# Reordering the last gates, halving the first attention input, and idle products at the start of a two-stage fp32/bf16 layer

## The reference

```
x = x + mamba_block(norm(x))      # norm, rmsnorm, in_proj, conv, scan with 16 states, gate, out_proj, FFN
x = x + gated(norm(x))            # recurrence over the 8 entries of the batch, then tanh
x = x + attention(norm(x))        # 16 heads of width 16; scores = (x_h W_h) x_h^T / 4
x = x + gated(norm(x))            # same weights as the first

def gated(x):                     # x[b] is 512 x 256, b = 0..7 in order
    for b in range(8):
        f, i = sigmoid(x[b] wf + c uf + bf), sigmoid(x[b] wi + c ui + bi)
        c = f * c + i * tanh(x[b] wc + c uc + bc)
    return tanh(x wo + c uo + bo)  # c is the last state
```

## Time and profile before

| | us |
|---|---|
| median of 3 runs | 1643.46 |
| lowest, highest | 1641.68, 1645.18 |
| profiled execution | 1647.02 |
| span of the profiled execution (first to last instruction) | 1645.2 |

### The profile page before, as it was taken

The page is one execution under the profiler, slowest core; times in us unless marked ns, Lnnn a source line. Parts: engine busy times, 40 slices in busy tenths (PEclk is TensorE's granted clock), DMA queues, the critical chain, the costliest instruction groups (busy, mean ns, idle before and its releaser), DMA issues.

```text
span 1645.2 us, 17272 instructions
## 1 busy us (share of the span) xinstructions
PE 1373.9 (84%) x5520; PEld 661.9 (40%) x5520; DVE 1183.2 (72%) x1824; ACT 884.9 (54%) x1512; POOL 689.7 (42%) x402
## 2 busy tenths in 40 slices
PE   4224789999999998999837989999999999989994
PEld 1102344545353635465411334444444443434442
DVE  3598898989898988950249777676767676666325
ACT  4664858585857574522211565646465555545533
POOL 2577879787878776730343121212030212100000
PEclk9666889999999999999965999999999999999997
DMA  5516060606161515100344433323243332320044
GB/s 177 179 40 205 28 230 28 230 28 217 41 205 53 192 53 179 52 32 8 102 95 100 73 95 78 79 54 86 57 97 73 84 76 55 85 53 15 15 157 137
DMA packets 93786, 158.04 MB, mean 96 GB/s; under 512 B 8592, under 2 KB 74704, under 8 KB 90576
## 3 DMA queue, kind: packets, MB, share of 16 engines
q1 hardware_dynamic: 93696, 156.94, 33.1%
HBM read 110.91 MB, written 46.01 MB: 95 GB/s over the span
## 4 chain that ended last, share of the span: by engine, by line
PE 62%; DVE 20%; issue 10%; ACT 4%; POOL 2%; DMA 1%; SPq 0%; DVEq 0%; POOLq 0%; ACTq 0%
PE psum L973 25%; PE psum L1860 8%; PE psum L1794 7%; PE psum L1768 7%; PE psum L1743 6%; PE psum L1783 5%; DVE psum L538 5%; DVE mx L1284 4%; PE psum L1018 2%; DVE middle L500 1%; DVE hb L538 1%; DVE stats L1260 1%; DVE hb L541 1%; PE psum L1738 1%; DVE bg_stats L468 1%
## 5 line engine op out<-in xcount | busy, mean ns | idle before, releaser
L1284 DVE TENSOR_REDUCE mx<-psum 128x1 f32<-128x512 f32 x512 | 344.9, 687 | 192.6 <-PE psum L1768 189.6
L1535 ACT ACTIVATE pw<-psum 128x512 f32<-128x512 f32 x512 | 301.9, 598 | 303.5 <-PE psum L1783 300.8
L910 POOL TENSOR_TENSOR hb<-ddb,bcb 128x1024 f32<-128x1024 f32 x128 | 309.8, 2443 | 65.5 <-DVE middle L500 52.3
L538 DVE TENSOR_TENSOR_SCAN psum<-psum,hb 128x512 f32<-128x512 f32 x224 | 261.5, 1213 | 29.7 <-ACT psum L729 18.1
L1768 PE MATMUL psum<-kp,qp 96*128 96x512 bf16 x512 | 209.2, 410 | 48.8 <-DVE mx L1284 30.0
L729 ACT ACTIVATE psum<-ddb,A_neg 128x512 f32<-128x512 f32 x256 | 165.4, 682 | 79.7 <-DVE hb L541 60.2
L1783 PE MATMUL psum<-qp,kp 99*128 99x512 bf16 x512 | 199.6, 391 | 7.8 <-ACT pw L1535 6.2
L1679 POOL TENSOR_TENSOR rstd<-rstd,neg_half 128x4 f32<-128x4 f32 x16 | 16.3, 1018 | 448.9 <-DVE rstd L1269 448.9
L541 DVE TENSOR_TENSOR hb<-psum,bcb 128x1024 f32<-128x1024 f32 x112 | 137.2, 1225 | 3.9
L1794 PE MATMUL psum<-pw,v_sb 128*32 128x512 f32 x1024 | 133.3, 641 | 0.5 <-ACT pw L1535 0.5
L973 PE MATMUL psum<-back,w 128*128 128x512 f32 x256 | 115.3, 605 | 8.3 <-ACT back L745 8.3
(11 more groups left out here) (189 smaller groups left out, 2166.9 us busy)
## 6 DMA issues: line engine op xcount, KB each, us to landing
ddb<-dd SPq DMA_DIRECT2D x64, 512.0 KB, 6.7
bcb<-bc SPq DMA_DIRECT2D x32, 512.0 KB, 6.7
parts<-parts_sb SPq DMA_DIRECT2D x96, 128.0 KB
dd<-dd_out SPq DMA_DIRECT2D x8, 1024.0 KB, 4.8
qp<-parts SPq DMA_DIRECT2D x32, 256.0 KB, 8.0
kp<-parts SPq DMA_DIRECT2D x16, 384.0 KB, 4.5
x_front<-x_dram SPq DMA_DIRECT2D x8, 512.0 KB, 4.2
xh<-x_front SPq DMA_DIRECT2D x8, 512.0 KB, 5.6
```

The lines of the kernel that those rows point to most:

```text
L538: e.tensor_tensor_scan(to[:, g, :], a[:, g, :], h[:, g, :], 0.0, ALU.mult, ALU.add).then_inc(scan_ok, 1)
L910: e.tensor_tensor(hb[n % NHB], ddb[k % NSLOT][:, 1:2, :].to_broadcast([P, 2, L]), bcb[q][:, 0, :, :], ALU.mult).then_inc(bx_ok, 1)
L1284: used.up(e.tensor_reduce(mx[u % 2][:, n:n + 1], bank(used.n % 2), AXIS.X, ALU.max))
L1535: e.activation(pw[n % NPW], bank(5 + n % 2), ACT.Exp, scale=HD ** -0.5).then_inc(exp_ok, 1)
```

## The change

There are four groups of edits.

1. Last gates. In round 8 the product gc of entry 6 comes after both halves of `back_second` in place of before them (TensorE, the ring's order, and VectorE, whose `gate_in` moves from u = 11 to u = 14 behind `back_new`). In round 9 `gate_xwo` of entry 7 is no longer ahead of the gates: its first half follows gf, its second half follows `final_state`; `last_gate_in` makes gi with the x terms of both halves first. ScalarE's copies and SP's store follow, so that the last `xwo1` store is issued in stage two, between `x_load(0)` and `x_load(1)`.
2. First attention input. `final_state` writes banks 0 and 1; cuo, xw, tanh, x2 and its moments of entry 0 go in two halves of two token tiles each. The wait for stage one's last stores moves behind them (`first_free`, and the end of `first_tanh`).
3. First q and k parts. All four steps of each (k, q) x (f = 0, 1) are done on VectorE in the order k0, q0, k1, q1 (`first_parts`), and SP sends and fetches one f after the other: 6 sends of f = 0, fetch(0), 6 sends of f = 1, fetch(1). GpSimd does none of them; its `front_bias(0)` and `restart` move into p = -2.
4. Idle products. `stay_warm(n)` does n fp32 products of 128 x 512 into bank 4, used by nothing: 8 at the very beginning, 2 after z of entry 0, 18 after dt of entry 0.

```
 # first_uses
-        if gate:
+        if gate and i != NB:
             use("dve", "gc", i - 2, 2)
         if back:
             use("dve", "ffn_out", i - 1, 2)
+        if gate and i == NB:
+            use("dve", "gc", i - 2, 2)
         if gate:
             use("dve", "gf", i - 2, 2)
+        if i == NB + 1:
+            use("act", "xwo", i - 2, 2)
...
 # pe_first
+            def stay_warm(n):
+                for _ in range(n):
+                    e.matmul(bank(4), ident, rows_flat[:, 0:L], start=True, stop=True)
+            def last_gate_in(b):
+                ring_out(e, "gturn", b, 1)
+                w = lambda f: slice(D + f * P, D + (f + 1) * P)
+                for f in range(NF):
+                    ring_free(e, "gi", b, f)
+                    for j in range(NF):
+                        e.matmul(ring("gi", b, f), wx[:, j, w(f)], feat(X0)[:, j, :], start=j == 0, stop=False)
+                e.wait_ge(c_new, b)
+                for f in range(NF):
+                    for j in range(NF):
+                        ins = e.matmul(ring("gi", b, f), uh[:, j, w(f)], c_state[:, j, :], start=False, stop=j == NF - 1)
+                    ins.then_inc(r_pe, 1)
+            stay_warm(8)
...
+                if i == -1:
+                    stay_warm(2)       # after mid_in z
...
+                if i == -1:
+                    stay_warm(18)      # after mid_dt
...
-                if gate:
+                if gate and i != NB:
                     gate_one(i - 2, "gc", 2)
...
+                if gate and i == NB:
+                    gate_one(i - 2, "gc", 2)   # after back_second(i - 1, 1)
                 if gate:
                     gate_one(i - 2, "gf", 0)
+                if i == NB + 1:
+                    ring_free(e, "xwo", i - 2, 0)
+                    token_product(ring("xwo", i - 2, 0), 0, feat(X0), wo).then_inc(r_pe, 1)
...
 # sp_second
+            def first_send(f):
+                for n in (1, 0):
+                    for c in range(3):
+                        if f == 0:
+                            e.wait_ge(first_part, 3 * (1 - n) + c + 1)
+                        elif c < 2:
+                            e.wait_ge(cast_ok, (0 if n else 2) + c + 1)
+                        else:
+                            e.wait_ge(sub_ok, 2 if n else 4)
+                        e.dma_start(part_dram[0][n, f, c]..., parts[n][:, c, f]).then_inc(part_sent[2 * n], 16)
             x_load(0)
+            ring_out(e, "xwo", NB - 1, 1)
+            e.dma_start(rows_of(xwo1_dram[NB - 1]), tok(G2)).then_inc(xwo1_sent[(NB - 1) % 2], 16)
             x_load(1)
-            for p in range(-4, NU):
+            for f in range(NF):
+                first_send(f)
+                fetch(f)
+            for p in range(-2, NU):
...
 # dve_second
             for u in range(2):
+                tiles = slice(2 * u, 2 * u + 2)
                 e.wait_ge(cuo_pe, u + 1)
-                e.tensor_tensor(cuo[:, 2 * u:2 * u + 2, :], halves(bank(5 + u)), ...).then_inc(cuo_ok, 1)
+                e.tensor_tensor(cuo[:, tiles, :], halves(bank(u)), ...).then_inc(cuo_ok, 1)
+                e.wait_ge(cuo_ok, u + 1)
+                e.wait_ge(xwo_in[0], 16)
+                e.tensor_tensor(xw[0][:, tiles, :], xw[0][:, tiles, :], cuo[:, tiles, :], ALU.add).then_inc(xc2_ok, 1)
...
+            def first_parts(n, f):
+                src, left = feat(A1 if n else A2)[:, f, :], feat(H1 if n else H0)[:, f, :]
+                misc_out(e, ("turn" if n else "q", 0, f))
+                ...
+                done(e.tensor_copy(part(0), src), cast_ok)
+                ins = e.tensor_tensor(left, src, part(0), ALU.subtract)
+                done(e.tensor_copy(part(1), left), cast_ok)
+                done(e.tensor_tensor(part(2), left, part(1), ALU.subtract), sub_ok)
...
                 if p == -3:
-                    first_cast(1, 0)
-                    first_cast(1, 1)
-                    first_cast(0, 0)
-                    first_sub(1)
-                    first_cast(0, 1)
-                    first_sub(2)
+                    for f in range(NF):
+                        first_parts(1, f)
+                        first_parts(0, f)
...
 # pool_second
+                if p == -2:
+                    front_bias(0)              # after front_xw(1)
...
-                if p == -3:
+                if p == -2:
                     restart()
...
 # pe_second
-            final_state((5, 6))
+            final_state((0, 1))
+            ring_free(e, "xwo", NB - 1, 1)
+            token_product(ring("xwo", NB - 1, 1), 1, feat(X0), wo).then_inc(r_pe, 1)
```

More of the change, by code:

```diff
@@ L402, in sp_first @@
                     e.dma_start(x_back, x_tile(b)).then_inc(x_back_in, 16)
-                if gate:
+                if gate and i <= NB:
                     ring_out(e, "xwo", i - 2, 1)
@@ L619, in dve_first @@
                         gated(i, 0)
-                    if u == 11 and gate:
+                    if u == 11 and gate and i != NB:
                         gate_in(i - 2)
@@ L623, in dve_first @@
                         back_new(i - 1)
+                    if u == 14 and i == NB:
+                        gate_in(i - 2)
                     if u == 15 and gate:
@@ L800, in act_first @@
                         gate_turned(i - 2)
-                    if u == 2 and gate:
+                    if u == 2 and gate and i <= NB:
                         gate_xwo(i - 2)
@@ L842, in act_first @@
                         gate_f(i - 2)
+                    if u == 15 and i == NB + 1:
+                        ring_done(e, "xwo", i - 2, 0)
+                        e.activation(tok(G2)[:, 0:2, :], halves(ring("xwo", i - 2, 0)), ACT.Copy).then_inc(r_act, 1)
                     if u == 15 and front:
@@ new lines, in first_stats, with first_free @@
+            def first_stats(k):
+                e.wait_ge(own.sem, own.n)
+                spread(x2[0], 0, k)
+            def first_free():
+                for i in range(2):
+                    e.wait_ge(x1_sent[i], 16 * NB // 2)
+                    e.wait_ge(xwo1_sent[i], 16 * NB // 2)
+            def first_parts(n, f):
+                src, left = feat(A1 if n else A2)[:, f, :], feat(H1 if n else H0)[:, f, :]
+                misc_out(e, ("turn" if n else "q", 0, f))
+                part = lambda c: parts[n][:, c, f, :]
+                done = lambda ins, sem_: ins.then_inc(first_part if f == 0 else sem_, 1)
+                at = (first_part, 3 * (1 - n)) if f == 0 else (cast_ok, 0 if n else 2)
+                done(e.tensor_copy(part(0), src), cast_ok)
+                e.wait_ge(at[0], at[1] + 1)
+                ins = e.tensor_tensor(left, src, part(0), ALU.subtract)
+                if f == 0:
+                    own.up(ins)
+                    e.wait_ge(own.sem, own.n)
+                else:
+                    ins.then_inc(sub_ok, 1)
+                    e.wait_ge(sub_ok, 1 if n else 3)
+                done(e.tensor_copy(part(1), left), cast_ok)
+                e.wait_ge(at[0], at[1] + 2)
+                done(e.tensor_tensor(part(2), left, part(1), ALU.subtract), sub_ok)
@@ L1622, in act_second @@
                         cast(b + 2, 0, 0, s - 18)
-                    if s == 19 and not odd and front:
+                    if s == 19 and not odd and front and b + 2 > 0:
                         front_tanh(b + 2)
+                    if s == 19 and p == -4:
+                        first_tanh()
                     if s == 22 and odd and gate:
```

99 lines of the change are left out of this document (47 added, 52 removed).

## The result

| | before | after |
|---|---|---|
| median of the runs, us | 1644.32 (1641.68 to 1647.71, 4 runs) | 1629.08 (1627.25 to 1631.91, 4 runs) |
| profiled execution, us | 1647.02 | 1629.72 |
| its span, us | 1645.2 | 1627.9 |

The ratio after to before is 0.9904, with a 95% interval of 0.9887 to 0.9920: 0.96% faster, 15.2 us by the medians. Forecast was 1626, a gain of 17.05.

A forecast was written before the change was run, and what follows sets the result against it. Chains of waits in the opening and the joint of the two stages, with PE mostly idle, bound the edited places. -4.6 - 2.45 - 1.5 + 0.3 - 9.3 + 0.5 = -17.05 took the median 1643.46 to 1626; range 1620 to 1636.

The forecast's parts named there:

- Opening: Start to entry 1's transposition: idle products raise the clock, so transposition, input products and xp run faster, -4.6 us.
- rival (a): Opening: clock not up at entry 0's transposition, by late products or a short idle time; opening gains 0, 1631; chance 0.09.
- (d): Opening: clock stays slow throughout, so the idle products are in the way; slower, 1648.6; chance 0.04.
- +0.95: Round 8: moving gc of entry 6 uncovers the last relu, PE waits before `back_second`, nothing won; +0.95 us.
- -3.4: Round 9: taking xwo from the front removes 5.0 us, but gi inherits 1.6 of slow clock; -3.4 us.
- Halves: Final state to T, start of the first attention input's transposition: work in two halves on VectorE shortens it; -1.5 us.
- the counted 0.3: Before T: VectorE waits for the last xwo1 store before writing the normalized input; +0.3 us.
- Parts and fetch: T to first score: parts on VectorE alone, f = 0 sent and fetched first; 18.8 us for 28.1, -9.3.
- 7.0 + 0.5: Fetch of f = 0: 7.0 us from q's first issue to landing, plus 0.5 for six sends queued behind.
- rival (b): Fetch bound by bytes and sends, not the queue behind; 5.5 for 9.3, store landing late 1.4; 1631.6; chance 0.08.
- Restart: Behind the first score: `restart` on GpSimd runs beside entry 1's normalization on VectorE; +0.5 us, bounds 0 and +3.
- Rival (c): First unit's scores: something else is late and takes the gain back; 1635.7, or 1638.9 for the whole joint; chance 0.07.

The follow-up runs named there:

- the best version: Kernel after with gc of entry 6 ahead of `back_second` again and idle products: 3 before the last gate transposition, 6 before T, 9 before the first score; 1624.37 us, ratio 0.9881.
- The kernel that holds everything back: Kernel after, but SP holds the six sends of f = 1 until all of q of f = 0 has landed; 1629.96 us, ratio 0.9913.

## Why the prediction was right

**Opening: right in size and in place.** -4.67 for -4.6. By the rule of the Trainium skill (TensorE: Matmul & The Clock Gate, Part 1: The HAM clock gate) the number of slow matmuls at a start varies, and its largest number would have given 3.5. Here about 6 of the first block were slow, fewer than the 8 to 10 that I took. That starts vary is borne out: in the twelve profiles with this block it took 8.62 to 10.21 us, so 4 to 8 of the 16 were slow, and it was always done before the transposition, by 0.38 to 2.89 us. In two of the twelve the input products behind the transposition then ran partly slow, and entry 1's transposition came at 59.5 in place of 58; these are the two with the longest waits ahead of the transposition, 2.29 and 2.89 us. So it looks as if rival (a)'s mechanism, a short idle time that drops the clock, did come in these two, for 1.5 us. The timelines of the best version, twice:

```profile
21.62 8.80 PE L986 MATMUL psum<-front,w_in 128*128 128x512 f32 x16 [1.01 <-ACT front L669]
```

```profile
21.71 7.10 PE L986 MATMUL psum<-front,w_in 128*128 128x512 f32 x16 [1.01 <-ACT front L669]
```

The 18 products, cost nothing and bring nothing: right. For the kernel after rivals (a) and (d) fell.

**Last gates: the step that failed is the price of moving gc, "+0.95".** What the uncovered relu costs was right (+1.04, in the timeline after as PE's wait of 0.78 us):

```profile
757.12 1.13 PE L990 MATMUL psum<-w,back 128*128 128x256 f32 x4 [0.78 <-ACT gate L760]
```

But the move has a second price that the prediction put at nothing, the clock behind PE's last wait. In the kernel after the last transposition was slow (1.69 for 1.09), and so were about six of gi's eight x products, (6.07 - 3.43) / 0.43. The clock was at the lower level until it rose between 794 and 796:

```profile
790.00:792.00 2.00, 1.96 (x3) 0.93 (x4) 0.00 (x0) 0.00 (x0) 0.26 (x1) 0.50 0.00 0
...
794.00:796.00 2.00, 2.00 (x5) 0.76 (x4) 0.00 (x0) 0.00 (x0) 0.00 (x0) 0.79 0.03 8
```

The order of gc decides it. In all six profiles with gc moved that transposition took 1.57 to 1.69, in the three with gc at its old place and nothing added to the wait 1.09. With gc back gi took 5.19, about four of the eight slow, that is 1.76 us of slow clock where I had let it inherit 1.6, and the final state came 26.92 behind the transposition in place of 30.33: 3.41 less. So the "-3.4" for taking xwo away was right by itself. Moving gc cost 1.04 + 1.42 = 2.46 for the forecast 0.95, and the two together brought 0.95 us for 2.45. With three idle products in the wait gi took 3.70. PE's wait ahead of the transposition is 2.74 us with gc in either place; why the order of the same products before it changes the clock behind it wasn't taken apart and stays open.

**Halves: right.** -1.67 up to T, for -1.2 with the store. The store of xwo's half landed at 822.37 + 3.37 = 825.74, just when VectorE had its normalization ready to start (825.96), so the counted 0.3 did not appear:

```profile
825.96 1.38 DVE L1336 TENSOR_SCALAR attend<-x,mv,rstd 128x256 f32<-128x256 f32 x4 [1.39 <-POOL rstd L1762]
```

No run has the halves alone. In the kernel with the idle products alone, which lacks them, the final state to T took 13.14, in the kernel after 11.48.

**Parts and fetch: the direction right, the size 1.7 too large.** The chain of copies was right: last send at T + 7.73 (7.9), landed at T + 11.1 (11.3). The step that failed is the fetch's 7.0 + 0.5, read from the fetch at 904.69 because that "had none behind it". From q's first issue at 838.63 to the first score it took 9.37 us, as before (9.4); that was rival (b)'s mechanism, at a third of its price, since the store landed in time and the six sends cost nothing. My argument had been that seven fetches queued behind q cost 2.4 us. The kernel that holds everything back shows that q takes as long with nothing behind it, 9.59. The trace of the kernel before had a row that said so too, which I did not look at: the fetch at 974.57, with k 1.28 us ahead of it and nothing behind it for 20 us, took 7.5 and not 6.4. SP's timeline and the answer on its DMA issues (KB each, median us to landing):

```profile
974.57 1.81 SPq L1192 DMA_DIRECT2D qp<-parts  x4
996.39 0.38 SPq L1215 DMA_DIRECT2D x_after_attention<-x  x1
```

```profile
qp<-parts SPq DMA_DIRECT2D x2, 256.0 KB, 7.5
```

What the fast fetch of the earlier trace rows had was another thing: k well ahead of it. SP had issued k's three pieces at 900.85, 3.8 us ahead of q at 904.69, where k's pieces of f = 0 went out only 2.8 us ahead of q. The kernel after has both cases as well. SP's timeline, and below it two answers on DMA issues (KB each, median us to landing), of the q fetch at 891.01 and of that at 920.99:

```profile
886.27 1.50 SPq L1249 DMA_DIRECT2D kp<-parts  x3
891.01 1.69 SPq L1249 DMA_DIRECT2D qp<-parts  x4
...
919.72 1.23 SPq L1249 DMA_DIRECT2D kp<-parts  x3
920.99 1.81 SPq L1249 DMA_DIRECT2D qp<-parts  x4
```

```profile
qp<-parts SPq DMA_DIRECT2D x2, 256.0 KB, 6.1
...
qp<-parts SPq DMA_DIRECT2D x2, 256.0 KB, 7.9
```

With k 4.7 us ahead q's pieces took 6.1, with k 1.3 us ahead 7.9, and in the fetch of f = 0, with 2.8, they took 7.6:

```profile
qp<-parts SPq DMA_DIRECT2D x2, 256.0 KB, 7.6
```

So it is what is still in flight ahead of q that delays it, k's 0.75 MB, and not what stands behind. All sixteen q fetches of the kernel after say the same: fifteen had k less than 3 us ahead and took 7.4 to 8.5, the one with 4.7 took 6.1. It is read from traces; an edit that sends k earlier wasn't tried. While the fetch of f = 0 lands, the DMA engines are full, with 168 GB/s:

```profile
840.00:842.00 2.00, 0.00 (x0) 0.00 (x0) 1.02 (x4) 0.00 (x0) 2.00 (x1) 1.00 1.09 168
```

So the engines' time for k and q seems to bound it, and not the number of bytes alone: in the stretch 844.05 to 848.05 of the best version, above, the same engines moved 222 GB/s at a share of 0.72.

**Restart: right to 0.2.** Unit 0's last maxima were written 32.7 us behind the first score, 32.4 before. Two of the four normalizations took 1.08 together in place of 0.73, beside the second GpSimd instruction of 1.6; the other two lay wholly beside the first, from 861.79 to 862.56, and took 0.77 for 0.73:

```profile
861.40 3.22 POOL L1758 TENSOR_SCALAR c_state<-c_state,in_c 128x512 f32<-128x512 f32 x2
...
863.08 1.08 DVE L1336 TENSOR_SCALAR attend<-x,mv,rstd 128x256 f32<-128x256 f32 x2
```

By the rule of the Trainium skill (SBUF — State Buffer, Who interferes with whom) as the prediction applied it, two of them would each have been blocked for most of such an instruction, +2 to +3 us in all. That full wait isn't borne out beside `restart`. Whether these normalizations run in a two-port mode, as the rule asks, no run shows. Beside a GpSimd addition of two tensors the same kind of normalization did wait as by that rule, 2.19 us for two, in the same trace. The 3.24 that the prediction took as agreeing was of that sort too, a subtraction of two tensors beside GpSimd's additions.

```profile
985.98 2.35 POOL L1773 TENSOR_TENSOR x<-x,xw 128x1024 f32<-128x1024 f32 x1
...
986.61 2.19 DVE L1336 TENSOR_SCALAR second<-x,mv,rstd 128x256 f32<-128x256 f32 x2
```

**Not predicted: -2.3 behind the first score, where +0.5 was forecast.** Without the 2.3 the trace would have given 15.0, as the medians do. That its 17.30 comes so near the forecast 17.05 is luck: the last gates brought 1.5 too little and the fetch 1.7 too little, and 2.8 of that came back here.

The distance from the first score to the end lay between 778.9 and 784.7 us in the fourteen traces, with nearly the same instructions in all of them. Most of that spread needs no edit: the best version had 783.8 in one profile and 779.1 in the other, the same program both times (the kernel after had 779.90 and 780.66). What differs is where the granted clock dips between units. The same 5 us of the best version in its two profiles, about 100 us behind the first score (columns as above):

```profile
945.00:950.00 5.00, 3.00 (x8) 0.73 (x9) 4.63 (x8) 2.30 (x5) 0.50 (x1) 0.69 0.13 34
```

```profile
945.00:950.00 5.00, 4.97 (x28) 1.38 (x27) 3.32 (x7) 3.38 (x7) 4.20 (x2) 1.00 0.43 135
```

What sets the places of these dips is open. Rival (c), a gain given back later, did not come for the change. With gc back the 2.5 us were gone by the end of its one profile, which the two of the best version show to be within what the dips alone do.

## What to carry to other kernels

Count a moved or removed product at the clock that its place will have afterwards: reordering the work ahead of a wait can make the work behind the wait slow. Here moving gc took no work away and cost 2.5 us, 1.4 of them through the clock, and three idle products in the wait brought 1.5. Cut transfers by what must land first and what must be sent before it, not by what is queued behind: fetching the first half alone gave 4.8 us, clearing the queue behind it gave 0. And take a transfer's time from several rows of its kind, and look in each at what was in flight ahead of it.

## What the runs showed of the hardware

- Full clock at the first score did not last: 1.00 in the 4 us before it and 0.55 in the 4 us after, while PE was busy for 3.1 of 4 us. Scores bounded by the row maxima stayed near the lower level (0.59 over 20 us); one idle product behind every score raised that to 0.84, two to 1.00.
- The same second stage took 778.9 to 784.7 us, and one and the same program 783.8 and 779.1, with the clock dipping at other places; that is more than most of the single edits here bring, and it hides them in a median.
- Of the first block of 16 instructions 4 to 8 were slow in twelve profiles (8.62 to 10.21 us), and in two of them some of the products 13 us later were slow again (8.69 and 8.80 for 7.10).
- A normalization on VectorE ran nearly unhindered beside GpSimd's tensor_scalar (0.77 for 0.73, two of them) and waited for GpSimd's addition of two tensors (2.19 for 0.73).
